# Layer norm on VectorE: two broadcast tensor products per piece, or eight instructions with partition scalars

## What is computed

```python
def _L1_conv_ref(x, w_hidden, w_dw, norm_w, norm_b, w_out, patch_size):
    hidden = jnp.einsum('oc,bchw->bohw', w_hidden, x)
    hidden = lax.conv_general_dilated(hidden, w_dw, ..., feature_group_count=w_dw.shape[0])
    q, k, v = jnp.split(hidden, 3, axis=1)
    ...
    out = jnp.fft.irfft2(q_fft * k_fft, s=(p, p))
    out = out.transpose(0, 1, 2, 4, 3, 5).reshape(b, c2, h, w)
    mu = out.mean(axis=1, keepdims=True)
    var = out.var(axis=1, keepdims=True)
    out_norm = (out - mu) / jnp.sqrt(var + 1e-05)
    out_norm = out_norm * norm_w[None, :, None, None] + norm_b[None, :, None, None]
    gated = v * out_norm
    return jnp.einsum('oc,bchw->bohw', w_out, gated)
x = x + _L1_conv_ref(_gn(x), ..., 8)
```

## Time and profile before

| what | value |
|---|---|
| median of 3 runs | 2822.24 us (2814.06 to 2825.8) |
| profiled execution | 2816.64 us, of which 2814.8 us span |
| granted clock, mean | 0.969 of full |
| PE, DVE, ACT, POOL busy | 89%, 59%, 51%, 17% of the span |
| first stage | up to about 560 us |
| one unit | 69.5 us where nothing disturbs it |

### The profile page before, as it was taken

How to read it: one execution, slowest core, us unless ns; L and a number is a source line. 1 busy time by engine, 2 the same in 40 slices (tenths; PEclk the granted TensorE clock), 3 DMA queues, 4 the chain that set the end, 5 groups by cost and what they waited for, 6 DMA issues and landing times.

```text
span 2814.8 us, 95766 instructions
## 1 busy us (share of the span) xinstructions
PE 2501.0 (89%) x40199; PEld 1660.3 (59%) x40199; DVE 1651.3 (59%) x4058; ACT 1439.9 (51%) x2381; POOL 466.5 (17%) x322
## 2 busy tenths in 40 slices
PE   7888888699898999898989998999899989999998
PEld 3333333466666666666666666666666666666665
DVE  4666666455555555555555555555555555555565
ACT  3555656555555555554555555545555554455552
POOL 1000000012121212121212121212121212121221
PEclk9988989799999999999999999999999999999999
DMA  6688978622222222222222222222222222222222
GB/s 128 174 228 213 233 203 214 162 59 66 64 64 63 61 61 65 61 60 61 66 62 66 64 67 61 62 61 65 62 66 64 65 62 60 59 62 61 66 56 46
DMA packets 60403, 249.11 MB, mean 88 GB/s; under 512 B 12393, under 2 KB 12658, under 8 KB 53714
## 3 DMA queue, kind: packets, MB, share of 16 engines
q1 hardware_dynamic: 59954, 242.50, 35.2%
HBM read 140.74 MB, written 101.72 MB: 86 GB/s over the span
## 4 chain that ended last, share of the span: by engine, by line
PE 59%; DVE 11%; issue 6%; ACT 3%; DVEq 0%; SPq 0%; ACTq 0%; DMA 0%
PE bank L654 16%; PE bank L577 12%; PE bank L670 9%; PE bank L637 7%; PE bank L590 6%; PE bank L558 6%; PE bank L599 4%; ACT arena L820 3%; DVE arena L1122 2%; DVE arena L1134 2%; DVE arena L1099 2%; DVE arena L1109 2%; DVE arena L1141 2%; DVE arena L1129 1%; ACT arena L865 0%
## 5 line engine op out<-in xcount | busy, mean ns | idle before, releaser
L441 POOL TENSOR_TENSOR arena<-arena 128x8 f32<-128x8 f32 x256 | 442.3, 1728 | 1827.6 <-DVE arena L1115 1817.5
L811 ACT ACTIVATE arena<-bank 100x512 f32<-100x512 f32 x1024 | 614.8, 628 | 227.4 <-PE bank L558 209.8
L577 PE MATMUL bank<-arena 128*64 128x512 f16 x4608 | 711.9, 400 | 7.6 <-issue 4.3
L1199 DVE TENSOR_TENSOR arena<-bank,arena 128x512 f32<-128x512 f32 x512 | 354.3, 692 | 438.4 <-PE bank L654 412.5
L558 PEld LDWEIGHTS bank<-arena 128*36 128x36 f16 (+1 forms) x8192 | 334.1, 106 | 423.2 <-issue 126.9
L558 PE MATMUL bank<-arena 128*36 128x128 f16 (+1 forms) x8192 | 406.7, 224 | 170.3 <-DVE arena L1099 127.2
L654 PE MATMUL bank<-arena 100*64 100x128 f32 x8192 | 510.0, 274 | 7.6 <-DVE arena L1199 7.6
L654 PEld LDWEIGHTS bank<-arena 100*64 100x64 f32 x8192 | 455.7, 136 | 45.4 <-issue 37.3
L512 PE MATMUL bank<-arena 32*32 32x508 f32 (+1 forms) x9216 | 386.8, 654 | 52.6 <-issue 37.7
L820 ACT ACTIVATE arena<-bank,arena 128x256 f32<-128x256 f32 x512 | 261.6, 561 | 172.0 <-PE bank L590 169.4
L1134 DVE TENSOR_TENSOR arena<-arena,bank 128x512 f32<-128x512 f32 x256 | 175.9, 687 | 286.3 <-ACT arena L820 284.8
(11 more groups left out here) (112 smaller groups left out, 1587.0 us busy)
## 6 DMA issues: line engine op xcount, KB each, us to landing
arena<-xn_d SPq DMA_DIRECT2D x128, 536.2 KB, 8.1
xn_d<-arena SPq DMA_DIRECT2D x130, 260.0 KB, 4.5
x_d<-arena SPq DMA_DIRECT2D x64, 512.0 KB, 8.3
arena<-x_d SPq DMA_DIRECT2D x128, 256.0 KB, 4.7
out<-arena SPq DMA_DIRECT2D x128, 256.0 KB, 5.3
arena<-x_in SPq DMA_DIRECT2D x32, 544.0 KB, 9.9
arena<-x_in SPq DMA_DIRECT2D x32, 528.0 KB, 9.7
arena<-spectra_in SPq DMA_DIRECT2D x1, 1152.0 KB
```

What stands on the lines that cost most here:

```text
L441: pool.tensor_tensor(tiny["rstd"][:, slot], tiny["var_eps"][:, slot], powers, ALU.pow).then_inc(s_root, 1)
L577: mm = pe.matmul(v_banks[chunk % 3][64 * s:64 * s + 64, :], v_w[:, 64 * tap:64 * tap + 64], at(xs[half], row * WP + 32 * k + dx, [32 * WP, ...
L811: act.activation(h_rows[0:WIN, :, first:first + 4], banks[g % ring][0:WIN, :].rearrange("p (i c) -> p c i", i=4), ACT.Copy).then_inc(s_h_r ...
L1199: dve.tensor_tensor(parts(prod[m % 4][:, 512 * second:512 * second + 512]), parts(k_banks[n % 3]), q_sb[m % 2][:, 256 * second:256 * secon ...
```

## The change

The copy of the means, `centre` and `scale` go, with two semaphores and the tile of the means. In their place `normalise` issues eight `tensor_scalar` a piece, one for each pixel column: 64 words at a stride of 32, in place, minus the column's mean and times its root, both read as a scalar per partition, the mean straight from what `bn_stats` wrote. DVE's order in `front` is written anew with it. The order on the other engines is the same.

```diff
@@ -1114,19 +1110,15 @@
                 dve.tensor_scalar(T["var_eps"][:, slot], at(T["pixel_stats"], 24 * (p % 4) + 2, [3, 8]), 1.0 / 64, EPS, ALU.mult,
                                   ALU.add).then_inc(s_var_eps, 1)
-                dve.tensor_copy(T["pixel_mean"][:, slot], at(T["pixel_stats"], 24 * (p % 4) + 1, [3, 8])).then_inc(s_pixel_mean, 1)
-
-            def centre(u, p):
-                piece = Y4[:, :, :, 4 * p:4 * p + 4]
-                dve.wait_ge(s_pixel_mean, 8 * u + p + 1)
-                dve.tensor_tensor(piece, piece, over(T["pixel_mean"][:, 8 * (p % 4):8 * (p % 4) + 8]), ALU.subtract).then_inc(s_y_centred, 1)
-
-            def scale(u, p):
-                piece = Y4[:, :, :, 4 * p:4 * p + 4]
+
+            def normalise(u, p):
                 dve.wait_ge(s_root, 8 * u + p + 1)
-                dve.wait_ge(s_y_centred, 8 * u + p + 1)
-                slot = slice(8 * (p % 4), 8 * (p % 4) + 8)
-                dve.tensor_tensor(piece, piece, over(T["rstd"][:, slot]), ALU.mult).then_inc(s_y_norm, 1)
+                for s in range(2):
+                    for j in range(4):
+                        pixels = at(Y, 2048 * s + 4 * p + j, [32, 64])
+                        i = 8 * (p % 4) + 4 * s + j
+                        ins = dve.tensor_scalar(pixels, pixels, T["pixel_stats"][:, 3 * i + 1:3 * i + 2], T["rstd"][:, i:i + 1], ALU.subtract, ALU.mult)
+                ins.then_inc(s_y_norm, 1)
@@ -1166,25 +1158,19 @@
                     pixel_stats(tail, p)
                     variance(tail, p)
                     if p == 1:
-                        centre(tail, 0)
-                scale(tail, 0)
-                windows()
-                centre(tail, 1)
-                scale(tail, 1)
-                windows()
+                        windows()
                 for p in range(8):
+                    normalise(tail, p)
                     if p < 5:
                         pixel_stats(tail, p + 3)
                         variance(tail, p + 3)
-                    if p < 7 or u is None:
-                        gate(tail, p // 2, p % 2)
-                    if p < 6:
-                        centre(tail, p + 2)
-                        scale(tail, p + 2)
-                    if p in (2, 4, 6):
+                    if p > 0:
+                        gate(tail, (p - 1) // 2, (p - 1) % 2)
+                    if p in (3, 5, 7):
                         residual(tail, p // 2 - 1)
-                    if p > 0:
-                        windows()
+                    windows()
+                if u is None:
+                    gate(tail, 3, 1)
```

More of the change, by code:

```diff
@@ L184, in build @@
         s_pixel_stats = semaphore("pixel_stats")
-        s_pixel_mean = semaphore("pixel_mean")
-        s_y_centred = semaphore("y_centred")
         s_var_eps = semaphore("var_eps")
@@ L235, in build @@
         powers = take(8)
-        tiny = {n: take(c) for n, c in (("v_scale", 1), ("v_shift", 1), ("pixel_stats", 96), ("pixel_mean", 32), ("var_eps", 32), ("rstd", 32))}
+        tiny = {n: take(c) for n, c in (("v_scale", 1), ("v_shift", 1), ("pixel_stats", 96), ("var_eps", 32), ("rstd", 32))}
         phases = top[0]
@@ L1087, in _ @@
                 first_stats(later, range(3, NCH))
-            Y4 = Y.rearrange("p (s c j) -> p s c j", s=2, j=32)
-            over = lambda a: a.rearrange("p (s j) -> p s j", s=2).unsqueeze(2).broadcast_to([128, 2, 64, 4])
             def window(u, half, r, b=None):
```

## The result

The changed kernel takes 2873.6 us (median of 4, 2869.16 to 2877.89), the kernel before 2822.64 in the runs beside it: a ratio of 1.0193, with a 95% interval of 1.0166 to 1.022. The forecast was 2864. The profiled execution has a span of 2867.3 us, 52.5 more than before. First the page of the changed kernel: busy time by engine, and the last chain.

A forecast was written before the change was run, and what follows sets the result against it. DVE was no bound on the average, but PE, busy 89%, waited in the fronts for its windows and scaled pieces. 16 x 0.95 + 15 x 1.55 + 3.5 gave +42 us, 2864 us on the median; range 2822 to 2950.

The forecast's parts named there:

- The price of a column: DVE's `normalise`: 0.257 us per 64-element instruction, so a piece costs 0.59 us more, 4.7 us more DVE work a unit.
- The low end: Pace of 0.224 us per instruction on DVE, at two elements a cycle; a piece then costs 0.32 us more.
- The path in a plain front: Plain front: turn 2 comes 5.0 us late, ended window waits return 4.3, gate 3 adds 0.25: +0.95 us.
- the wait of 0.25 for gate 3: Plain front, behind turn 2: gate 3 is late next, and project 1 waits 0.25 us for it.
- The front that begins a pass: Window 2 waits for group 3 ahead of piece 0; turn 0 is 1.88 us late, costing 1.55 on the average.
- The last tail: Last unit's tail, no PE work to hide in: eight pieces add 4.7 us, a quarter covered by ACT waits: +3.5.
- The clock rival: PE's clock falls after turn 0's longer wait, 1.4 us each, 31 fronts: 43 us more, 2907; chance 0.08.
- The sum: Whole kernel: 16 plain fronts at 0.95, 15 pass-beginning ones at 1.55, last tail 3.5: +42 us.
- The cheap column: Rival on DVE's instruction: stride free, two elements a cycle, +8 or +2 us, 2815 to 2836; chance 0.22.
- the heavy one: Rival on DVE's instruction: one element a step, stride costs a second cycle, pace 0.32, 2890 to 2980; chance 0.2.
- Faster: Rival: early windows end 127 us of PE waits, late gate 1 costs less; at pace 0.18, 2792; chance 0.08.
- both halves: Plain front: early windows end PE's window waits, returning 4.3 us; gate 1 comes late, putting turn 2 5.0 late.

The follow-up runs named there:

- the filler: Changed kernel with 18 useless products on PE ahead of turn 0 in 15 plain fronts: 2857.45 us, ratio to before 1.0128.
- order_only: Changed kernel's new DVE order, but with the old centre, scale and copy of the means: 2800.25 us, ratio to before 0.9932.
- n0_first: Changed kernel with piece 0 scaled ahead of window 2 and the statistics of piece 2: 2826.83 us, ratio to before 1.0034.
- fused_best: The order of early_both with `normalise` in place of each centre and scale: 2749.96 us, ratio to before 0.9747.
- ops_only: Kernel before, in its old DVE order, with `normalise` in place of centre and scale: 2953.38 us, ratio 1.0455.
- early_windows: Kernel before, old instructions, with windows 4 to 7 moved ahead and residual 1 one piece earlier: 2684.25 us, ratio 0.9524.
- early_both: early_windows with piece 0 ahead of window 2 and piece 2's statistics, residual 0 ahead of window 6, windows 6 and 7 one piece earlier: 2674.27 us, ratio 0.9484.

## Why the prediction was right, step by step

**The price of a column.** Taken 0.257, measured 0.245 to 0.257 in the kernel and 0.244 alone. The low end was 0.224, which is what neighbouring words cost. The split was right too: two scalars 0.12, the stride one element a cycle in place of two. The choice rested on no strided row, and was in part luck.

**The path in a plain front.** The front with PE at full clock is that of the filler, where nothing else differs. Its Y is complete at 1528.91. Turn 0 at +5.66 (5.65 predicted), turn 1 at +10.55 (10.57), v chunk 3 at +12.11 (12.15), turn 2 at +18.28 (18.3). The waits for windows went as predicted, and the unit grew from 69.52 to 70.3, by 0.77 in place of 0.95. Turn 2 is on time, so the difference lies behind it: the wait of 0.25 for gate 3, ahead of project 1, does not come. The chain from window to piece to gate to turn is what made the loss, and the waits that went paid for most of it.

**The front that begins a pass.** 1.55 predicted. Turn 0 was to start at +7.17, and in the eight of these fronts without a fall of the clock ahead of it it starts at +7.06 to +7.39. What was too large is how late that is. The prediction took one front of before, with turn 0 at +5.29. That is nearly the earliest: the ten without a fall ahead of turn 0 are at +5.78 on the average, so turn 0 is 1.4 late and not 1.88. Accordingly the units without any fall grew from 70.81 (nine) to 71.80 (five), by 1.0. Over all 14 the growth is 1.78, from 71.05 to 72.83; the rest of it goes with the clock, which fell 13 times in them after the change and 5 times before. That 1.78 lies near 1.55 is luck.

**The last tail.** 31.6 us from complete Y to the last residual's end before, 35.1 after: +3.5, as predicted.

**The step that was mis-sized is the clock.** The prediction had it as a rival at 0.08, "if as often as the gaps, about 8", and left it at nothing in the sum. It came in 16 of 17 plain fronts, 1.1 to 1.2 us each: 18 us. Eight more falls than before came in the fronts that begin a pass, about 11 us by the lengths above. In the other direction went five falls behind waits for windows in plain fronts, whose units took 71.1 us where the others took 69.5: 8 us.

**The sum.** Without the clock the runs give 17 x 0.77 + 14 x 1.0 + 3.5, some 30 us, where the prediction had 42; the clock adds nearly 20. Together that is the 48 us by which the second stage of the profiled execution grew. The other 4.2 of its 52.5 were there already when the first tail started, which no part of the change touches. So the chain and its places were right, and that 42 came so near to 51 is in part luck: fronts that were priced too dear made up for a clock that was priced at nothing.

**The rivals.** The cheap column and the heavy one are out by the measured pace. "Faster" is out for the change, but its mechanism was sound: early windows with the old pieces and an undisturbed gate 1 are worth 5%. The clock rival (2907, a fall in each of 31 fronts) had the mechanism right for the plain fronts and the size too large. The prediction saw both halves and priced them; it did not ask what the first half was worth alone.

## What to carry to other kernels

Where a list of instructions on one engine serves two consumers, place each item where its input comes free, not in the rhythm of a loop: moving four window copies (and one residual by one place) was worth 132 us here, and one copy and one piece's statistics ahead of the first scaled piece cost 45. A fused instruction saves passes over the data but pays its fixed part on each call: eight calls with two scalars per partition (1.96 to 2.06 us) were dearer than two whole products (1.39). And a wait on TensorE can cost more than its length, since the clock may be lower behind it. Filling it with other products took the falls at that place away here, and so did an order that cut it to 0.98 us; cutting it from 2.90 to 2.25 did not.

## What the runs showed of the hardware

- A `tensor_scalar` of 64 fp32 goes by in 0.102 us with immediates and in 0.222 with two scalars per partition: each such scalar costs 0.05 to 0.06 us.
- Single words at a stride of 32 are read at about one element a cycle and neighbouring ones, or pairs at that stride, at two, for a cycle of about 1 ns (128 for 64 elements: 71 and 34 ns more; pace of 64: 0.244, 0.222 and 0.224 us). Writing them at that stride costs nothing more (0.222).
- PE's clock can fall to 1.2 GHz at or just behind the first products that follow a wait. At turn 0 in the 17 plain fronts it did so 16 times after a wait of 2.90 us, 15 after 2.53 (`order_only`), 16 after 2.25 (`n0_first`), 14 after 2.26 (`fused_best`), but once after 2.37 (`ops_only`). After 1.84 it was once before the change and 9 times in `early_windows`, and after 0.98 (`early_both`) never, nor after 0.92 in the 15 filled fronts. So at turn 0 no fall followed a wait under 1 us (in four filled fronts one came 7 us later, behind the 0.88 and 0.85 us ahead of turn 1 and v chunk 3), and for the longer waits the length alone does not say whether the clock falls. One fall cost 1.1 to 1.2 us of time at turn 0 in the changed kernel, 1.3 in `early_windows` and 1.6 behind the window waits of the kernel before.
- POOL's roots held nothing back in the changed kernel. Where piece 0 stands right behind the statistics of piece 1 (`n0_first`, `fused_best`) DVE waits 0.77 us for the root in each tail, 24.6 us in all.
